# A token tower with a product-key memory: other slots for tile search and both attentions, and the keys masked by head on ScalarE

## The reference

```python
h = tokens(x) @ W + b                          # wavelet maps, resized to 8 x 8
h = concatenate([cls_tok, h], axis=1)          # 64 images x 65 tokens x 64
# block 1: cosine attention, 8 heads of 8 channels
q, k, v = split(layernorm(h) @ qkv_w.T + qkv_b)
attn = softmax(unit(q) @ unit(k).T * scale + bias)
h = h + (attn @ v) @ proj_w.T + proj_b
# block 2: each token reads a table of 4096 rows per head by product keys
s = query @ pk_keys                            # two sides of 64 scores
s0, s1 = top16 of each side                    # 16 x 16 sums
w, idx = top16 of the sums; w = softmax(w)
k, v = sum(w * keys_table[idx]), sum(w * values_table[idx])
h = h + (softmax(causal(query2 @ k.T)) @ v) @ Wo      # 8 heads
```

## Time and profile before

| | us |
|---|---|
| median of 3 runs | 2952.06 |
| the profiled execution | 2948.71 |
| its span, first to last instruction | 2946.9 |
| TensorE busy in it | 2853.7 |
| VectorE busy | 2512.6 |
| ScalarE busy | 1769.7 |
| GpSimd busy | 1586.5 |

### The profile page before, as it was taken

How to read it: one execution, slowest core, us unless ns; L and a number is a source line. 1 busy time by engine, 2 the same in 40 slices (tenths; PEclk the granted TensorE clock), 3 DMA queues, 4 the chain that set the end, 5 groups by cost and what they waited for, 6 DMA issues and landing times.

```text
span 2946.9 us, 60045 instructions
## 1 busy us (share of the span) xinstructions
PE 2853.7 (97%) x16560; PEld 1976.2 (67%) x16560; DVE 2512.6 (85%) x10266; ACT 1769.7 (60%) x4888; POOL 1586.5 (54%) x3427
## 2 busy tenths in 40 slices
PE   8899999999999999999999999999999999999998
PEld 7867766666666666666666666666666666777776
DVE  4678889998899889988998899989998998788876
ACT  4466666565656656665566565655566666666665
POOL 2234456665666556655666566656665665343331
PEclk9999999999999999999999999999999999999999
DMA  9213211112111211121212111211121111101100
GB/s 219 55 47 82 54 30 32 33 34 43 29 33 34 41 26 33 34 42 30 34 34 41 32 33 34 40 33 33 34 39 33 34 35 35 26 21 27 26 21 19
DMA packets 121290, 117.48 MB, mean 40 GB/s; under 512 B 61491, under 2 KB 109310, under 8 KB 120958
## 3 DMA queue, kind: packets, MB, share of 16 engines
q1 hardware_dynamic: 105525, 83.84, 13.5%
q0 software_dynamic: 14336, 29.39, 5.9%
q10 hardware_dynamic: 1096, 0.41, 0.1%
HBM read 66.36 MB, written 9.84 MB: 26 GB/s over the span
## 4 chain that ended last, share of the span: by engine, by line
PE 72%; DVE 18%; issue 5%; POOL 3%; ACT 2%; ACTq 0%; DMA 0%; DVEq 0%; POOLq 0%
PE ps L854 40%; PE ps L840 14%; DVE wts L1250 7%; DVE x_sum L1325 3%; PE ps L776 2%; PE ps L804 2%; PE ps L885 2%; PE ps L745 2%; PE ps L727 1%; PE ps L793 1%; PE ps L869 1%; ACT wts L1028 1%; PE ps L767 1%; DVE top L1234 1%; DVE cand_rest L1236 1%
## 5 line engine op out<-in xcount | busy, mean ns | idle before, releaser
L854 PE MATMUL ps<-wts,table 128*128 128x455 f32 (+2 forms) x5120 | 2004.9, 475 | 0.0
L1250 DVE SCALAR_TENSOR_TENSOR wts<-ps,wts 128x455 f32<-128x455 f32 (+2 forms) x2560 | 1346.3, 530 | 280.3 <-ACT wts L1028 266.6
L1028 ACT ACTIVATE wts<-ps 128x455 f32<-128x455 f32 (+2 forms) x2560 | 1179.3, 475 | 368.2 <-PE ps L840 346.0
L840 PE MATMUL ps<-st,spread 128*128 128x456 f32 (+2 forms) x2560 | 1288.6, 503 | 36.2 <-DVE wts L1250 28.5
L854 PEld LDWEIGHTS ps<-wts,table 128*128 128x128 f32 x5120 | 906.6, 190 | 141.4 <-issue 62.9
L840 PEld LDWEIGHTS ps<-st,spread 128*128 128x128 f32 x2560 | 483.9, 189 | 400.1 <-DVE wts L1250 268.5
L612 POOL DMA_INDIRECT x_rows<-folded,x_r x448 | 452.8, 1011 | 87.1 <-issue 78.7
L545 POOL TENSOR_SCALAR stat<-top 110x1 f32<-110x1 f32 (+1 forms) x268 | 70.0, 261 | 717.7 <-DVE top L1234 715.0
L532 POOL TENSOR_TENSOR cand<-best 110x15 f32<-110x15 f32 (+5 forms) x804 | 159.9, 226 | 178.1 <-DVE best L1218 176.6
L1325 DVE SCALAR_TENSOR_TENSOR x_sum<-iota,x_pf,x_at 128x69 f32<-128x69 f32 x448 | 179.3, 400 | 0.0
L804 PEld LDWEIGHTS ps<-ident,parts 110*128 110x128 f32 (+1 forms) x536 | 63.3, 141 | 139.4 <-issue 121.0
(11 more groups left out here) (188 smaller groups left out, 3839.2 us busy)
## 6 DMA issues: line engine op xcount, KB each, us to landing
st<-st SPq DMA_DIRECT2D x320, 114.0 KB
table<-in_table SPq DMA_DIRECT2D x128, 128.0 KB, 4.4
rz_row<-rz_dram SPq DMA_DIRECT2D x52, 165.0 KB
folded<-table SPq DMA_DIRECT2D x64, 128.0 KB, 2.6
x_rows<-folded,x_r POOLq DMA_INDIRECT x448
rz_row<-rz_dram SPq DMA_DIRECT2D x28, 228.0 KB
scratch<-in_x SPq DMA_DIRECT2D x7, 343.0 KB
rz_dram<-rz SPq DMA_DIRECT2D x52, 1.3 KB
```

What stands on the lines that cost most here:

```text
L840: mm(ps[0:128, g % NA, 0:t], spread[:, q * 128:(q + 1) * 128], st[:, k % 2, ORDER[c // QUADS], 0:t], start=True, stop=True).then_inc(a_rea ...
L854: mm(ps[0:128, ACC + k % 2, 0:t], table[:, k % H, i, :], wts[:, g % RING, 0:t], start=(c == 0), stop=(c == CH - 1)).then_inc(out_done, 1)
L1028: A(wts[:, g % RING, 0:t], ps[0:128, g % NA, 0:t], ACT.Exp).then_inc(e_ready, 1)
L1250: V.scalar_tensor_tensor(out=wts[:, g % RING, 0:t], in0=ps[0:128, g % NA, 0:t], scalar=0.0, in1=wts[:, g % RING, 0:t], op0=ALU.is_ge, op1= ...
```

## The change

Nineteen numbers of slots are changed, and one operation goes to another engine. The product of the keys with a column of `head_of`, one number per channel, was a GpSimd tensor_scalar and becomes a ScalarE activation, a Copy with that column as its scale, in the same step -2 of a task. No matmul and no transfer is added or removed.

```diff
-OUT, BEST, CAND, TOP, SHIFT, ZSUM, HIGH, ZINV, LOW, TURN, TURNED = 2, (2, 3, 5), 6, 8, 13, 15, 15, 16, 16, 17, 19
+OUT, BEST, CAND, TOP, SHIFT, ZSUM, HIGH, ZINV, LOW, TURN, TURNED = 2, (3, 4, 5), 6, 7, 13, 15, 16, 15, 17, 18, 20
-X_OUT, X_BEST, X_CAND, X_INDEX, X_WHERE, X_TOP = 1, 2, 7, 8, 9, 9
+X_OUT, X_BEST, X_CAND, X_INDEX, X_WHERE, X_TOP = 1, 3, 7, 8, 9, 9
-X_GATHER, X_ADD, X_TURN, X_MOVE = 22, 30, 77, 78
+X_GATHER, X_ADD, X_TURN, X_MOVE = 23, 30, 77, 78
@@ GpSimd, front
-                j = task_at(p, q, -2)
-                if j is not None:
-                    pool.wait_ge(qk_unit, 2 * p + 2)
-                    if j >= 1:
-                        pool.wait_ge(s_mm, base + j)
-                    P.tensor_scalar(kx[0:C, 0:t], xf[:, 0:t], head_of[0:C, j:j + 1], None, ALU.mult)\
-                        .then_inc(kx_ready, 1)
@@ TensorE, front
-                j = task_at(p, q, 0)          # scores
+                j = task_at(p, q, -1)
-                j = task_at(p, q, 11)         # output
+                j = task_at(p, q, 9)
-                if q == after_tasks(p) + 3:   # projection
+                if q == after_tasks(p) + 2:
@@ TensorE, attend
-                if u == 6:                    # value turns
+                if u == 5:
-                if u == 13:                   # turns of the weights
+                if u == 12:
@@ ScalarE, front
-                j = task_at(p, q, 5)
+                j = task_at(p, q, -2)
+                if j is not None:
+                    act.wait_ge(qk_unit, 2 * p + 2)
+                    if j >= 1:
+                        act.wait_ge(s_mm, base + j)
+                    A(kx[0:C, 0:t], xf[:, 0:t], ACT.Copy, scale=head_of[0:C, j:j + 1]).then_inc(kx_ready, 1)
+                j = task_at(p, q, 6)          # exponential
@@ ScalarE, attend
-                if u == 8:                    # exponential
+                if u == 9:
@@ VectorE, attend
-                if u == 17:                   # addition to h_sb
+                if u == 18:
@@ VectorE, main loop
-                if k >= 1 and u == 1:
+                if k >= 1 and u == 2:
                     take_sum(k - 1)
```

## The result

The kernel after takes 2841.01 us (median of 4 runs, 2838.7 to 2842.92), the kernel before, run beside it, 2952.15: a ratio of 0.9623, 95% interval 0.9607 to 0.964, so 111 us less. A second comparison gave 0.9629 (0.9616 to 0.9642).

The account below looks back on a forecast made before the run. TensorE, busy 97% of the span, was taken as the floor, fed late in places. Gains of 49, 5.6, 3.5 and 3, together 61 us, less charges of 4 and 7, gave 50 us: 2902 us, range 2866 to 2944.

Parts of the forecast that it names:

- The turn's load: TensorE's weight load at a tile's turn waits for ScalarE's copy; about 6 us a pass lost, most of it taken away.
- the lookup beside the subtraction: VectorE's row lookup L1325 in D heads (all tokens through the table) takes 1.61 us beside GpSimd's subtraction; collision shrinks from 1.3 to 0.3.
- the threshold that ScalarE waited for: Tile search releases the threshold one slot sooner, so ScalarE's waits for it go, 0.57 us at one place.
- the exponential L1037: ScalarE's exp at slot 8 waited 0.89 us for GpSimd's subtraction and held the next exp; at slot 9 it does not.
- The 42 us off VectorE: Moved gathers let subtractions start earlier: 42 places at 1.0 us each, 42 us less on VectorE, bounds 0 and 56.
- The slower rival: First search step, now one slot behind the candidates, waits longer for GpSimd: 43 us on VectorE; +23 us, 2975; chance 0.11.
- the share of each head's excess that comes back: Of some 17 us a pass above TensorE's floor and open to other slots, 7.0 comes back, 49 us in 7 passes.
- more comes back than the places I count: Rival: 12 of the 17 us a pass come back in 7 passes, -85 us, 2867; chance 0.10.
- VectorE stays close behind: Reason for crediting D heads 2 and 4 only 1.2 us each of their 1.9 us excess.
- VectorE's picks at 18 to 23 remain: Reason for crediting S heads (327 columns) 3 and 5 only 0.7 us each of their 3.0 us excess.
- The charges of 4 and 7 us: Costs subtracted: 4 us for the key product on ScalarE, 7 us for new waits from the attention slots in 80 heads.
- The key product: Rival: GpSimd's key product held 28 VectorE lookups about 1 us each; half reaches the end, -14 more, 2888; chance 0.03.

Follow-up runs that it names:

- b_search: Only the tile search steps and take_sum moved, against the kernel before: 2905.06 us, ratio 0.9849.
- b_attn: Only the slots of both attentions changed, keys still on GpSimd, against the kernel before: 2924.73 us, ratio 0.9917.
- b_keys: Only the product of the keys moved from GpSimd to ScalarE, against the kernel before: 2939.72 us, ratio 0.9983.
- S, G and A: Tile search with take_sum (S), gathers (G) and attention slots (A) changed together, against the kernel before: 2856.08 us, ratio 0.9676.
- v2: Kernel after with one token activation for four, layer norm turns and query/key a slot later, unit products split over two slots: 2838.84 us, ratio 0.9637 to before.
- a_gather: Kernel after with only the gathers put back from slot 23 to 22: 2876.06 us, ratio 0.9752 to before.
- b_gather: Only the gathers moved one slot later, from 22 to 23, against the kernel before: 2965.21 us, ratio 1.0054.

## Why the prediction was wrong

**What bounds the kernel: right.** TensorE was the floor, VectorE fed it late; both in the chain (18% to 2%) and in the waits for the mask (268.5 to 132.9 us).

**The places: right.** The turn's load, the lookup beside the subtraction, the threshold that ScalarE waited for and the exponential L1037 were all found in the profile of before, and all four waits are gone or small. The 42 us off VectorE were 42 us, but the prediction gave them to the gathers, and alone these take 20; the rest needs the tile search with them. No run takes ZINV or take_sum by itself; that they cost nothing was not contradicted. The slower rival's wait for candidates fell in after, and in b_search it grew as that rival said.

**The step that failed: the share of each head's excess that comes back.** The prediction put the excess open to other slots at 17 us a pass and credited 7.0 of it: 1.2 each for heads 2 and 4, 0.7 each for 3 and 5, 0.9, 0.9, 0.5 and 0.9 for 0, 1, 6 and 7. Measured by the windows, in the same order (2 and 4, 3 and 5, then 0, 1, 6, 7): 1.9 and 1.6, 2.1 and 2.0, 1.6, 0.0, 1.1, 2.6. That is 12.9 a pass in place of 7.0, over seven passes 90 in place of 49. The last pass gave 7.2 in place of 5.6; pass 0 and 8 gave 8.1 in place of 6.5. Together, with the 0.9 ahead of the first table product, 106 and not 61. The rival "more comes back than the places I count" (12 of the 17, chance 0.10) had this term nearly right; it still subtracted the costs and had less in the other passes, so its 2867 is too slow as well.

Two sentences carried the small credit, and both fell. "VectorE stays close behind": it is busy 37.37 of 39.00 us in head 2 of after, and TensorE is busy all through; its load queue waits for the mask 1.2 us there, 0.4 at the longest. VectorE at 96% did not hold TensorE there; that the three PSUM banks and four buffers cover what is left is a reading, since no run changes their number. "VectorE's picks at 18 to 23 remain": they do, and the S heads gave 2.0 each all the same. Their excess came from the late threshold and from L1037, not from the picks: from one head's first table product to the next head's, heads 3 and 5 take 33.9 and 34.3 us in before, 32.6 and 33.1 with the search alone (b_search, whose waits for the threshold fall from 99.2 us to 11.8), and 33.1 and 33.6 with the attention slots alone (b_attn, where L1037 waits 0.5 us in place of 33.4). That is 1.3 and 0.7 of the 2.0.

**The charges of 4 and 7 us: not there.** Keys on ScalarE gain 5 (b_keys), where 4 were charged, and the attention slots gain 24 to 25 from either end, where the prediction names 7 as their cost, and the exponential that no longer holds the next one as their gain, without a number. Without these charges its own sum is 61.

**The gathers: right in after, wrong as a part.** The prediction saw only that the gather leaves the place before L571 and not which place it takes: in S heads the one behind the threshold, where it makes the whole cost 16 us unless the threshold is early. The five alone add up to 24 + 45 + 25 + 5 - 16 = 83, which is already more than 61; the pair of search and gathers adds 42, and some 15 go again, most of them at the turn (24 alone, 11 on top of S, G and A).

**The sum of the parts.** The places were added one by one with a discount on each, as if every place could at best bring its own part. But the late starts of a head cover each other: mend one, and the next is what TensorE waits for. For search and gathers the waits above show it (the exponential, the lookups, the candidates); for the others it is read from the sums. Removing one group from after costs 16 + 37 + 24 + 61 + 3 = 141 us in sum, more than the 110 that all give. Parts that only added up would give the same sum.

**The key product.** That rival's full block of lookups beside the product did not show: b_keys is worth 5 us where the rival had 14, on 28 lookups at about 1 us each. The 14 lookups that do stand beside it in before lose 1.5 us in all, and in b_keys VectorE's stretch is 59.0 us where it was 61.6.

## What to carry to other kernels

When a pipelined kernel is near its floor in busy time but far from it in its chain, put a bound on a re-slotting by the whole gap to the floor of each stretch, beside the sum of discounted waits. Here the whole gap was 17 us a pass, 12.9 came back and 7.0 were forecast: nearly all of the gap in D heads, two thirds in S heads, none in head 1. Ask for each stretch what would still be late if all named waits were gone. Price what is moved by the place it takes as well as by the one it leaves, in each kind of iteration by itself. And test slots in pairs: the gathers cost 16 us alone and were worth 37 at the end.

## What the runs showed of the hardware

GpSimd's power of 65 x 7 numbers took 1.52 us and that of 65 x 5 took 1.20, so 0.16 us a column, beside 0.95 for the subtraction of 65 x 455. Four activations of 64 x 56 took 0.35 each (1.40), one of 64 x 224 took 0.66 in v2. Seven turns of 64 x 64 (L866) take TensorE 0.55 us to the start of what follows, in all 56 places of after, and seven of 65 x 65 (L728) 0.39, the smaller ones the longer; why is open.

In a_gather the lookup's record begins 0.75 us before the subtraction's (1053.76 and 1054.51), and it ends 0.12 us after it (1055.59 and 1055.47, start plus duration); a lookup is otherwise over in 0.28. A gather (1053.39 to 1054.48) filled the time before. It is the subtraction that holds the lookup and not the gather: in before, 71 lookups stand beside a gather and nothing else, and none takes over 0.02 us more than the median. In b_gather, 12 lookups of this kind begin 0.5 us before the other subtraction (L522), with no gather beside them, and take 1.6 us; VectorE, then GpSimd:

```profile
1094.41 1.57 DVE L1325 SCALAR_TENSOR_TENSOR x_sum<-iota,x_pf,x_at 128x69 f32<-128x69 f32 x1
```

```profile
1094.38 0.60 POOL L532 TENSOR_TENSOR cand<-best 110x32 f32<-110x32 f32 x3
1094.94 0.94 POOL L522 TENSOR_TENSOR scratch<-scratch,red 65x455 f32<-65x455 f32 x1
```

The Trainium skill, page "SBUF — State Buffer", section "Who interferes with whom", says that the order of issue decides who blocks, and not the shape of the operation. The records here do not bear that out: the lookup's starts first and yet it ends with the subtraction, and in the earlier trace rows the lookup that starts 0.32 us after the key product (a tensor_scalar of 64 x 455) loses 0.13 us and ends 0.73 before it. Whether a record's start is the moment of issue is not shown by any run.
